# Values of the second half's first two head pairs by seven products, and the routing cut into five parts

## The chip, the cores and the metric

One core of a Trainium2 chip. The metric is the device time of one execution in microseconds; the kernel before takes 2572.6 us (median of 3 runs, 2571.44 to 2572.82).

## The reference

Two layers on x of 8 sequences of 256 tokens, 512 wide, all in float32. What concerns this change is layer 0, whose attention and expert layer both read the layer norm of x:

```
xn  = layernorm(x)                                  # 2048 tokens x 512
q, k, v = silu(xn @ qkv_w.T)                        # 32 heads of 128
attn = scores(q, k) * decay, times v, per head      # causal, blockwise in the reference
gate = sigmoid(xn @ gate_w.T)
x1  = x + (gate * norm(attn)) @ out_w.T + experts(xn)
# experts: logits = xn @ router_w + router_b; softmax, + bias; 2 of 4 groups of 4 experts,
# then the 2 best of the 16 experts per token; each token's two experts are summed with their scores
```

Layer 1 (another attention and a sparse mixture of low-rank pieces) comes after and isn't touched.

## The kernel before

**Numbers.** Every float32 product is made of three passes (`three_passes`, lines 90 to 98: high by high, high by low, low by high), in which each operand is split into a rounded high part and the low rest. ACT makes the high part of a weight (`split`, a cast from `w_in` to `wh`), POOL the low part (`low`, L1805, from `w_in` and `wh` to `wl`). Pieces are 512 columns; a section of weights has four.

**Halves and pairs.** Layer 0's attention runs over two halves h = 0, 1 of 1024 tokens, and in each over 16 pairs of heads. A `Round` is the work for one pair: section 0 (its weights are called "q") makes q and k of the pair's first head, section 1 ("k") those of the second, section 2 ("g") the gate of both. Each section is seven products of a Strassen-Winograd scheme in the order ORDER = (1, 5, 6, 2, 7, 3, 4), each of six matmuls of 128x512 columns. The weights' sums for it are made by POOL (`add_up`, four operations, L492 to L498), and the products' sums by DVE: `summed(r, j, "c")` (L1565) is wanted by product 7 and `summed(r, j, "e")` (L1568) by product 4. ACT copies and activates the results (`take`: "ab", "t5", "a", "e", "c", "b").

**Values.** A regular double is an even and an odd round. In its even round the values of two pairs are made together, as sections 3 and 4 by the same seven products (each of 12 matmuls of 128x256; the weights are v0 and v1, brought by `bring_values` in two transfers each). Only the first double of each half was different: rounds "first" and "second" made their values straight, with `project_v`, four calls per pair of 24 matmuls of 128x256 each.

In half 1, "first" ran: section 0, with the router's matmuls (`route`, `by_token`) inside; project_v 0 and 1; section 1; section 2, with two matmuls for the routing (L1144, L1145: prefix sums and totals of the masks) after its fourth product; scores 0 and 1; project_v 2 and 3. "second" ran three project_v, the scores 0 and 1 and the last project_v at its end. Its v was brought and split for pair 0 at the end of half 0 and the begin of half 1, and q and k of pair 0 too; the gate's weights are brought when half 0's last output matmul is done.

**Order of the work.** Each engine has its program written out by hand in the functions `sync`, `tensor`, `scalar`, `vector` and `gpsimd` inside `half`, each with a `run(r)`; engines meet by counting semaphores, whose counts `Round` works out (`products`, `takes`, `adds`, `splits`, `sums`; `READY` says how many split pieces a section's matmuls wait for; `PLACE` which of four places in `w_in` a section's weights use).

**Routing.** DVE works it out in half 1 for all 2048 tokens, in chains of small operations (`Routing`, lines 136 to 301), each waiting for the one before: in "first", `scores`, (ACT: `exponentials`), `probabilities`, `choose`, `mask_groups` between the sums of section 0 and "c" of section 1; `masks` between "e" of section 1 and "c" of section 2; `count` (which reads the two matmuls' results) after "e" of section 2. In "second", `place` ahead of gated(2), `gates_of_choices` ahead of add_out(0), `experts_of_tiles` after add_out(1). `add_out` takes one of project_out's eight results from one of two banks, and project_out(t) waits for add_out(t - 2).

Of the kernel before, what the change touches and what calls it, by code (L numbers as in the profile page):

```python
# [11 lines left out]
ALU = mybir.AluOpType  # L12
# [121 lines left out]
class Routing:  # L134
# [90 lines left out]
    def count(self, v, prefix, totals):  # L225
# [3 lines left out]
        ab = [x[:, 0:n] for x in self.cmp]  # L229
        c.link(v.tensor_copy(ab[0], totals))  # L230
        incl, free = self.running(v, ab[0], ab[1], E, n)

# [3 lines left out]
        c.link(v.tensor_tensor(above, incl[:, n - E:n].unsqueeze(2).to_broadcast([P, E, NTHR]), thr, ALU.is_gt))  # L236
# [5 lines left out]
        c.link(v.tensor_scalar(tmp, tmp, float(SLOT_T), None, ALU.mult))  # L242
        self.slot = free.rearrange("p (t e) -> p t e", e=E)
# [4 lines left out]
        self.col = tmp  # L248

    def place(self, v, slot_of, ready):  # L250
        c = self.chain
        shape = "p (i t) -> p i t"
        s, col, tile, wrap = (x.rearrange("p t g -> p (t g)")[:, i * 2 * NT:(i + 1) * 2 * NT].rearrange(shape, i=2)
                              for x in (self.gm, self.keep) for i in range(2))
        for i, m in enumerate((self.m0, self.m1)):
            c.link(v.tensor_tensor(self.prod, m, self.slot, ALU.mult))
            c.link(v.tensor_reduce(s[:, i, :], self.prod, AX_X, ALU.add))
# [72 lines left out]

class Round:
# [8 lines left out]
    SPLIT = {"front0": {"v": 2, "q": 6, "k": 10, "g": 14}, "front1": {"q": 4, "k": 8, "v": 10, "g": 14},  # L340
# [3 lines left out]
    SUMMED = {"front0": {"q": 4, "k": 8, "g": 12}, "front1": {"q": 4, "k": 8, "g": 12}, "first": {"q": 4, "k": 8},  # L344
# [4 lines left out]
    PLACE = {"front0": {"q": 0, "k": 1, "g": 2, "v": 3}, "front1": {"q": 0, "k": 1, "g": 2, "v": 3},  # L349
# [3 lines left out]
    def __init__(self, kind, m=0):  # L353
        self.kind, self.m = kind, m
        self.front, self.first, self.second, self.even, self.odd, self.end = (
            kind.startswith(k) for k in ("front", "first", "second", "even", "odd", "end"))
# [3 lines left out]
        self.takes = self.since(0, 22, 44, 30, 48)  # L360
        self.adds = self.since(0, 6, 12, 10, 16)
        self.splits = self.since(14, 24, 40, 22, 36)
        self.sums = self.since(12, 20, 32, 20, 32)

    def since(self, first, second, third, even, both):
# [2471 lines left out]
```

## Time and profile before

| | |
|---|---|
| median of 3 runs | 2572.6 us |
| profiled execution, its time | 2570.18 us |
| its span | 2568.3 us |
| mean granted clock of TensorE | 0.991 |
| busy: PE, DVE, ACT, POOL | 97%, 46%, 45%, 59% |
| matmuls of the values, per pass (`wh,xh` 128x256) | 912 |
| PE's share of the chain that ended last | 85% |

Busy time of TensorE is that of pipelined matmuls, each of which overlaps the next; so a matmul's own duration (400 ns for 512 columns) is longer than the distance to the next one's start. Times in the timelines are microseconds from the span's start. An operation's bracket gives the engine's idle time before it and what ended that. Half 0 fills the time to about 1045 us, half 1 of the attention goes from there.

### The profile page before, as it was taken

Reading aid. Unit: us, or ns where it says so; the run is one execution under the profiler, and the core shown is the slowest. Engines: PE = TensorE matmul, PEld = TensorE weight load, DVE = VectorE, ACT = ScalarE, POOL = GpSimd, SP = SyncE. Lnnn points to the kernel's source line nnn. Section 1 sums busy time; section 2 is a strip of 40 time slices with the busy share of each in tenths; the row PEclk is TensorE's granted clock in tenths of the full one; section 3 lists DMA queues with packets and bytes.
Section 4 is the critical chain, followed back from the end, with each engine's and each line's share of the span. In section 5 each row is a group of like instructions: output and inputs, shape, how many; then the busy total and the mean of one; then the engine's idle time right before and its main releaser. Section 6 shows DMA issues by size and latency. Waiting matters only on the chain.

```text
span 2568.3 us, 39435 instructions
## 1 busy us (share of the span) xinstructions
PE 2495.5 (97%) x13338; PEld 2140.1 (83%) x13338; DVE 1172.4 (46%) x1937; ACT 1152.2 (45%) x2182; POOL 1508.9 (59%) x1523
## 2 busy tenths in 40 slices
PE   7999999999999999999999999999999999969999
PEld 6888888888888888778888888888888888857777
DVE  6333333434343435763334343434343588865443
ACT  5444444444444444443444444444444457733332
POOL 5756656666575754765666766757575578731210
PEclk9999999999999999999999999999999999979999
DMA  4211110111111112211111011111111178931100
GB/s 166 87 48 40 55 63 31 63 47 61 36 58 47 56 40 99 94 48 48 40 55 63 31 63 47 59 35 61 47 56 40 60 245 305 301 101 34 37 29 33
DMA packets 84950, 188.00 MB, mean 73 GB/s; under 512 B 12610, under 2 KB 30674, under 8 KB 84870
## 3 DMA queue, kind: packets, MB, share of 16 engines
q1 hardware_dynamic: 76326, 170.13, 20.0%
q0 software_dynamic: 8544, 16.82, 2.2%
q8 instruction: 48, 0.79, 0.1%
q14 instruction: 32, 0.26, 0.0%
HBM read 168.00 MB, written 26.79 MB: 76 GB/s over the span
## 4 chain that ended last, share of the span: by engine, by line
PE 85%; DVE 7%; ACT 4%; issue 2%; DMA 1%; POOL 1%; ACTq 0%; SPq 0%; DVEq 0%
PE bank L95 24%; PE bank L96 23%; PE bank L97 23%; PE bank L1081 4%; PE bank L1064 4%; PE bank L1082 2%; PE bank L1065 2%; DVE el L2201 2%; ACT exth L2161 1%; ACT eh L2172 1%; ACT eh L2166 1%; DVE ehf L2213 0%; DMA l_stage<-y_slots,slot_of 0%; POOL l_stage L2720 0%; PE bank L539 0%
## 5 line engine op out<-in xcount | busy, mean ns | idle before, releaser
L1805 POOL TENSOR_TENSOR wl<-w_in,wh 128x512 fp32r<-128x512 f32 x510 | 587.7, 1179 | 189.5 <-ACT wh L1348 183.2
L95 PE MATMUL bank<-xh,wh 128*128 128x512 f32 x1400 | 560.7, 400 | 0.7 <-ACT bank L1296 0.7
L97 PE MATMUL bank<-xh,wl 128*128 128x512 f32 x1400 | 546.6, 390 | 0.0
L1823 POOL TENSOR_TENSOR sqacc<-sqacc,sq 128x512 f32<-128x512 f32 x128 | 165.6, 1294 | 379.3 <-ACT sq L1333 368.2
L1348 ACT CAST wh<-w_in 128x512 fp32r<-128x512 f32 x502 | 263.6, 567 | 274.0 <-POOL w_in L498 274.0
L96 PE MATMUL bank<-xl_sums,wh 128*128 128x512 f32 x800 | 315.8, 395 | 0.0
L97 PEld LDWEIGHTS bank<-xh,wl 128*128 128x128 f32 x1400 | 263.0, 188 | 57.3
L95 PEld LDWEIGHTS bank<-xh,wh 128*128 128x128 f32 x1400 | 263.5, 188 | 53.4 <-ACT bank L1296 0.9
L1602 DVE TENSOR_TENSOR acc<-bank,acc 128x512 f32<-128x512 f32 x240 | 165.7, 691 | 299.6 <-PE bank L97 299.6
L95 PE MATMUL bank<-wh,xh 128*128 128x256 f32 x912 | 260.3, 285 | 3.3 <-DVE xl L550 3.3
L96 PE MATMUL bank<-wl,xh 128*128 128x256 f32 x912 | 258.4, 283 | 0.0
L96 PE MATMUL bank<-xl,wh 128*128 128x512 f32 x600 | 234.6, 391 | 0.0
L1559 DVE TENSOR_TENSOR ms<-bank,dcur 128x384 f32<-128x384 f32 x256 | 142.3, 557 | 154.4 <-PE bank L1065 145.2
L95 PE MATMUL bank<-oh,yh 128*128 128x512 f32 x512 | 200.7, 392 | 6.7 <-DVE acc L1600 5.3
L1577 DVE SCALAR_TENSOR_TENSOR yf<-gT,bank 128x512 f32<-128x512 f32 x128 | 88.0, 687 | 249.1 <-PE bank L1082 249.1
L96 PE MATMUL bank<-ol,yh 128*128 128x512 f32 x512 | 200.0, 391 | 0.0
L97 PE MATMUL bank<-oh,yl 128*128 128x512 f32 x512 | 199.8, 390 | 0.0
L1582 DVE SCALAR_TENSOR_TENSOR yl<-yf,little,yh 128x512 fp32r<-128x512 f32 x128 | 131.0, 1023 | 137.0 <-ACT yh L1338 134.8
L1565 DVE TENSOR_TENSOR bank<-bank,t 128x512 f32<-128x512 f32 x128 | 89.5, 699 | 195.3 <-PE bank L97 183.5
L95 PEld LDWEIGHTS bank<-wh,xh 128*128 128x128 f32 x912 | 174.5, 191 | 4.9 <-DVE xl L550 2.1
L96 PEld LDWEIGHTS bank<-xl_sums,wh 128*128 128x128 f32 x800 | 150.6, 188 | 29.6
L96 PEld LDWEIGHTS bank<-wl,xh 128*128 128x128 f32 x912 | 174.5, 191 | 0.7
(354 smaller groups left out, 5394.4 us busy)
## 6 DMA issues: line engine op xcount, KB each, us to landing
w_in<-in_w_pairs_dram SPq DMA_DIRECT2D x100, 512.0 KB, 3.8
o_in<-in_o_pairs_dram SPq DMA_DIRECT2D x32, 512.0 KB, 4.8
eraw<-in_ex_dram SPq DMA_DIRECT2D x31, 513.0 KB, 5.1
y_slots<-ey SPq DMA_DIRECT2D x31, 512.0 KB, 6.0
w_in<-in_w_pairs_dram SPq DMA_DIRECT2D x56, 256.0 KB, 3.1
dcur<-in_decay_dram SPq DMA_DIRECT2D x32, 384.0 KB, 3.0
eraw<-in_ex_dram SPq DMA_DIRECT2D x31, 256.0 KB, 5.1
out_dram<-acc SPq DMA_DIRECT2D x16, 256.0 KB, 2.0
```

The costliest lines, as they stand in the source:

```text
L95: pe.matmul(out, wh, mh, start=start and i == 0, stop=False, skip_group_check=True)
L96: pe.matmul(out, wh, ml, start=False, stop=False, skip_group_check=True)
L97: ins = pe.matmul(out, wl, mh, start=False, stop=stop and i == n - 1, skip_group_check=True)
L1064: pe.matmul(sc[i % 2][:, 0:S], kT[:, hd, s0:s0 + P], qT[:, hd, s0:s0 + S], start=True, stop=True)
L1081: pe.matmul(out, v0, ms[i % 2][:, 0:S], start=True, stop=False, skip_group_check=True)
L1348: a.copy(wh[:, cols], w_in[:, cols]).then_inc(w_hi, 1)
L1559: v.tensor_tensor(ms[i % 2][:], sc[i % 2][:, 0:MC], dcur[:, ITEMS[i][0], :], ALU.mult).then_inc(v_mask, 1)
L1565: v.tensor_tensor(pj[2][:], pj[1][:], t5[:], ALU.add).then_inc(v_c, 1)
L1582: v.scalar_tensor_tensor(yl[g % 2][:], yf[:], nwcur[:, g % 2:g % 2 + 1], yh[g % 2][:].bitcast(F32), ALU.mult, ALU.subtract).then_inc(v_yl, 1)
L1602: v.tensor_tensor(now[:, t, :], op[t % 2][:], now[:, t, :], ALU.add).then_inc(v_acc, 1)
L1805: pool.tensor_tensor(wl[:, cols], w_in[:, cols], wh[:, cols].bitcast(F32), ALU.subtract).then_inc(w_lo, 1)
L1823: pool.tensor_tensor(sqacc[:, c], sqacc[:, c], sq[:], ALU.add).then_inc(p_sq, 1)
```

## The change

In half 1 the rounds "first" and "second" are replaced by Round("even", 0, h=1) and Round("odd", 0, h=1), that is by a regular double with m = 0; half 0 keeps "first" and "second". So in half 1:

- TensorE: no project_v; section 1 directly after section 0; section 2, then section 3 (seven products for the values), products 1 and 5 of section 4, scores 0 and 1, the rest of section 4. The routing's two matmuls go after the fifth product of section 2, not the fourth. The odd round is a regular one.
- v is neither brought at the end of half 0 nor split at the start of half 1. SP brings v0 ahead of o_in, v1 when section 0 is done.
- ACT splits g after the copies "ab" and "t5" of section 1, v0 after "a" and "c" of section 1, v1 around "e" of section 2. POOL's order is: sums for g, sums for v0, low g, low v0, v1, o, token numbers, q, k.
- DVE: `count` is cut in three, and the slots' sum is taken out of `place`. `count_tiles` comes after "e" of section 2, `count_experts` between "c" and "e" of section 3, `count_slots` and `slots_of_choices` after "e" of section 3, `place` after "e" of section 4. In the odd round `gates_of_choices` and `experts_of_tiles` stand together where `place` stood, ahead of gated(2).

The diff, cut to its core:

```diff
-    def count(self, v, prefix, totals):
+    def count_tiles(self, v, totals):
+        ab = [x[:, 0:NT * E] for x in self.cmp]
+        self.chain.link(v.tensor_copy(ab[0], totals))
+        self.incl, self.free = self.running(v, ab[0], ab[1], E, NT * E)
+
+    def count_experts(self, v):
...
+        c.link(v.tensor_tensor(above, self.incl[:, n - E:n].unsqueeze(2).to_broadcast([P, E, NTHR]), thr, ALU.is_gt))
         c.link(v.tensor_reduce(tiles, above, AX_X, ALU.add))
         c.link(v.tensor_copy(ends, tiles))
         self.ends, tmp = self.running(v, ends, tmp, 1, E)
         c.link(v.tensor_tensor(tmp, self.ends, tiles, ALU.subtract))
         c.link(v.tensor_scalar(tmp, tmp, float(SLOT_T), None, ALU.mult))
+        self.col = tmp
+
+    def count_slots(self, v, prefix, totals):
...
         c.link(v.tensor_tensor(free, incl, totals, ALU.subtract))
         c.link(v.tensor_tensor(free, free, prefix, ALU.add))
         c.link(v.tensor_tensor(self.slot, self.slot, tmp.unsqueeze(1).to_broadcast([P, NT, E]), ALU.add))
+
+    def slots_of_choices(self, v):
...
+        for i, m in enumerate((self.m0, self.m1)):
+            c.link(v.tensor_tensor(self.prod, m, self.slot, ALU.mult))
+            c.link(v.tensor_reduce(self.places[0][:, i, :], self.prod, AX_X, ALU.add))
...
-        self.products = self.since(0, 25, 50, 35, 56)
+        self.products = self.since((0, 25, 50), 0, 35, 56)
...
     def ready(self, j):
-        return self.splits + self.READY[self.kind][j]
+        return self.splits + ((-4, 0, 4, 12) if self.first else self.READY[self.kind])[j]
...
             def all_rounds(eng, run):
-                run(FIRST)
-                run(SECOND)
+                run(Round("even", 0, h) if last else Round("first"))
+                run(Round("odd", 0, h) if last else SECOND)
...
             def sync(sp):
                     if r.even:
-                        wait(sp, pe_p, r.products)
+                        if not r.first:
+                            wait(sp, pe_p, r.products)
                         bring_values(sp, r, 0)
...
-                wait(sp, v_yl, 4 * UNITS + 4)
-                bring(sp, FRONT[1], "v", pair_section(0, "v"))
...
             def tensor(pe):
                         section(r, 0, *ORDER[3:])
-                        if last:
-                            project_v(r, 0)
-                            project_v(r, 1)
                         section(r, 1, *ORDER)
-                        section(r, 2, *ORDER[:4])
+                        section(r, 2, *ORDER[:5])
                         if last:
                             masks = router.lg.rearrange("p t e -> p (t e)")
                             wait(pe, v_masks, 1)
...
-                        section(r, 2, *ORDER[4:])
+                        section(r, 2, *ORDER[5:])
...
-                    if r.first and last:
-                        scores(r, 0)
-                        scores(r, 1)
-                        project_v(r, 2)
-                        project_v(r, 3)
-                        return
...
             def scalar(a):
                     if r.first and last:
                         router.exponentials(a)
-                        take_v(r, 0)
-                        take_v(r, 1)
...
                     take(r, 1, "ab")
-                    elif r.odd:
+                    elif r.odd or r.first and last:
                         split(r, "g", 0, 1)
...
                     take(r, 1, "t5")
-                    if r.first and last:
-                        split(FRONT[h], "g", 0, 1, 2, 3)
-                    elif r.odd:
+                    elif r.odd or r.first and last:
                         split(r, "g", 2, 3)
...
                     take(r, 1, "a")
+                    if r.first and last:
+                        split(r, "v0", 0, 1)
...
                     take(r, 1, "c")
+                    if r.first and last:
+                        split(r, "v0", 2, 3)
...
                     take(r, 2, "a")
+                    if r.first and last:
+                        split(r, "v1", 0, 1)
                     take(r, 2, "e")
+                    if r.first and last:
+                        split(r, "v1", 2, 3)
...
             def vector(v):
                         if last:
                             wait(v, pe_pre, 1)
-                            router.count(v, ot[:, 0:NT * E], op[0][:, 0:NT * E])
+                            router.count_tiles(v, op[0][:, 0:NT * E])
...
                         y_low(u, 1)
-                        if second and last:
-                            router.place(v, slot_of, v_slots)
+                        if r.routes:
+                            router.gates_of_choices(v, gate_of)
+                            router.experts_of_tiles(v, expert_of, gates, v_gates)
...
-                        if second and last:
-                            router.gates_of_choices(v, gate_of)
                         add_out(u, 0)
                         summed(r, 1, "c")
                         add_out(u, 1)
-                        if second and last:
-                            router.experts_of_tiles(v, expert_of, gates, v_gates)
...
                         summed(r, 3, "c")
+                        if r.first:
+                            router.count_experts(v)
                         summed(r, 3, "e")
+                        if r.first:
+                            router.count_slots(v, ot[:, 0:NT * E], op[0][:, 0:NT * E])
+                            router.slots_of_choices(v)
                     mask(n, 0)
                     mask(n, 1)
                     if r.even:
                         summed(r, 4, "c")
                         summed(r, 4, "e")
+                        if r.first:
+                            router.place(v, slot_of, v_slots)
...
             def gpsimd(pool):
+                    if r.first:
+                        add(r, "g")
+                        add(r, "v0")
+                        low(r, "g")
+                        low(r, "v0")
+                        add_low(r, "v1")
+                        low_o(r)
...
+                        add_low(r, "q")
+                        add_low(r, "k")
+                        return
...
-                if last:
-                    low(FRONT[1], "v")
-                add_low(FRONT[h], "g")
+                if not last:
+                    add_low(FRONT[h], "g")
```

## Rows read from the trace of the kernel before

**Rows 1.** The page: the span, and TensorE's line of busy times.
```profile
span 2568.3 us, 39435 instructions
PE 2495.5 (97%) x13338; PEld 2140.1 (83%) x13338; DVE 1172.4 (46%) x1937; ACT 1152.2 (45%) x2182; POOL 1508.9 (59%) x1523
```

**Rows 2.** Stretches: length; busy PE, PEld, DVE, ACT, POOL; clock, DMA, GB/s.
```profile
1098.00:1134.00 36.00, 29.90 (x138) 24.99 (x138) 29.27 (x55) 11.11 (x20) 18.75 (x19) 0.91 0.12 42
1166.00:1227.00 61.00, 61.00 (x336) 53.27 (x335) 21.45 (x31) 27.93 (x52) 41.44 (x41) 1.00 0.16 51
```

**Rows 3.** Waits of TensorE from 1045 to 1170 us: total, times, longest.
```profile
PE bank L95 <- DVE acc L1600: 5.3, 1, 5.3
PE bank L1081 <- DVE ms L1559: 0.8, 1, 0.8
PE bank L1144 <- DVE acc L213: 0.7, 1, 0.7
```

**Rows 4.** Timeline of TensorE: start, duration, what, [idle before, releaser].
```profile
1034.21 0.80 PE L95 MATMUL bank<-wh 128*128 128x512 f32 x1 [2.44 <-DVE acc L1755]
...
1061.19 0.28 PE L95 MATMUL bank<-wh,xh 128*128 128x256 f32 x1
...
1066.94 0.40 PE L95 MATMUL bank<-xh,wh 128*128 128x512 f32 x1
...
1082.91 0.70 PE L1144 MATMUL bank<-acc 128*128 128x256 f32 x2 [0.74 <-DVE acc L213]
...
1125.92 0.80 PE L95 MATMUL bank<-oh,yh 128*128 128x512 f32 x1 [5.29 <-DVE acc L1600]
...
1129.78 0.39 PE L95 MATMUL bank<-xh,wh 128*128 128x512 f32 x1
```

**Rows 5.** Timeline of VectorE (DVE), the routing's chains and add_out(0).
```profile
1063.82 0.42 DVE L181 TENSOR_REDUCE acc<-acc 128x16 f32<-128x256 f32 x1 [1.97 <-ACT acc L154]
...
1069.71 0.42 DVE L205 TENSOR_TENSOR acc<-acc 128x256 f32<-128x256 f32 x1
...
1074.62 0.41 DVE L162 TENSOR_REDUCE acc<-acc 128x16 f32<-128x256 f32 x1
...
1081.47 1.39 DVE L213 TENSOR_TENSOR acc<-acc 128x256 f32<-128x256 f32 x1
...
1091.08 0.71 DVE L236 TENSOR_TENSOR acc<-acc 128x128 f32<-128x128 f32 x1
...
1096.61 0.42 DVE L244 TENSOR_TENSOR acc<-acc,bank 128x256 f32<-128x256 f32 x1
...
1111.49 0.96 DVE L256 TENSOR_TENSOR acc<-acc 128x256 f32<-128x256 f32 x1
...
1115.46 0.18 DVE L263 TENSOR_SCALAR acc<-acc 128x32 f32<-128x32 f32 x1
1115.68 1.16 DVE L261 TENSOR_SCALAR acc<-acc 128x32 f32<-128x32 f32 x1
...
1120.76 0.69 DVE L1577 SCALAR_TENSOR_TENSOR yf<-gT,bank 128x512 f32<-128x512 f32 x1
...
1122.29 0.41 DVE L278 TENSOR_TENSOR acc<-acc 128x256 f32<-128x256 f32 x1
...
1125.18 0.69 DVE L1600 COPY acc<-bank 128x512 f32<-128x512 f32 x1
...
1126.98 0.17 DVE L283 COPY acc<-acc 128x16 f32<-128x16 f32 x1
...
1131.04 0.41 DVE L299 TENSOR_TENSOR logits<-acc 128x256 f32<-128x256 f32 x1
```

**Rows 6.** Timeline of GpSimd (POOL): low parts of a section, four operations.
```profile
1071.08 4.48 POOL L1805 TENSOR_TENSOR wl<-w_in,wh 128x512 fp32r<-128x512 f32 x4 [9.27 <-ACT wh L1348]
...
1115.48 4.53 POOL L1805 TENSOR_TENSOR wl<-w_in,wh 128x512 fp32r<-128x512 f32 x4 [0.73 <-ACT wh L1348]
```

**Rows 7.** Timeline of ScalarE (ACT): the casts of g's four pieces.
```profile
1070.38 1.97 ACT L1348 CAST wh<-w_in 128x512 fp32r<-128x512 f32 x4
```

More of the change, by code:

```diff
@@ L348, with __init__, since @@
     READY = {"second": (-6, 0, 4, 6), "even": (-6, -2, 4, 12), "odd": (-4, 0, 4), "end": (-6, -2)}
-    PLACE = {"front0": {"q": 0, "k": 1, "g": 2, "v": 3}, "front1": {"q": 0, "k": 1, "g": 2, "v": 3},
+    PLACE = {"front0": {"q": 0, "k": 1, "g": 2, "v": 3}, "front1": {"q": 0, "k": 1},
              "first": {"q": 0, "k": 1}, "second": {"g": 2, "v": 3, "q": 0, "k": 1},
              "even": {"g": 2, "v0": 3, "v1": 0, "q": 1, "k": 2}, "odd": {"g": 3, "q": 0, "k": 1}}
[L353 to L356, printed above, removed]
+    def __init__(self, kind, m=0, h=0):
+        self.kind, self.m, self.h = kind, m, h
+        self.front, self.second, self.even, self.odd, self.end = (
+            kind.startswith(k) for k in ("front", "second", "even", "odd", "end"))
+        self.first = kind == "first" or self.even and zero(m)
+        self.routes = self.odd and zero(m)
         self.n = UNITS if self.end else m * 2 + 1 if self.odd else m * 2 if self.even else int(self.second)
         self.u = self.n - 1
-        self.products = self.since(0, 25, 50, 35, 56)
[L360 to L365, printed above, removed]
+        self.products = self.since((0, 25, 50), 0, 35, 56)
+        self.takes = self.since((0, 22, 44), 0, 30, 48)
+        self.adds = self.since((0, 6, 12), 0, 10, 16)
+        self.splits = self.since((14, 24, 40), 8, 22, 36)
+        self.sums = self.since((12, 20, 32), 8, 20, 32)
+    def since(self, starts, again, even, both):
         if self.front:
@@ L369, in since @@
         if self.first:
-            return first
+            return again if self.h else starts[0]
         if self.second:
-            return second
+            return starts[1]
         if self.end:
-            return third + both * ((UNITS - 2) // 2)
-        return self.m * both + (third - both + (even if self.odd else 0))
+            return again + both * (UNITS // 2) if self.h else starts[2] + both * ((UNITS - 2) // 2)
+        return self.m * both + ((again if self.h else starts[2] - both) + (even if self.odd else 0))
     def last(self):
@@ L406, in section @@
         return j + (1 if self.odd else 0)
-FRONT = [Round(f"front{h}") for h in range(2)]
-FIRST, SECOND, END = (Round(k) for k in ("first", "second", "end"))
-def zero(n):
-    return isinstance(n, int) and n == 0
+FRONT = [Round(f"front{h}", h=h) for h in range(2)]
+SECOND = Round("second")
 def attention(nc, ctx, x_tiles, xn_dram, x1_dram, token_slots, w_pairs, o_pairs, decay, norm_w, router_w,
@@ L988, in product @@
                                 wait(pe, a_c, taken_n(r, "v", 0))
-                        elif j == 1 and r.first and last:
-                            wait(pe, a_c, taken_n(r, "v", 0))
                         else:
@@ L993, in product @@
                     if k == 5:
-                        if j == 1 and r.first and last:
-                            wait(pe, a_c, taken_n(r, "v", 1))
-                        elif j:
+                        if j:
                             wait(pe, a_c, taken_n(r, "c", j - 1))
@@ L1896, in run @@
                         send(0)
-                    if r.second and last:
+                    if r.routes:
                         pool.wait_ge(v_slots, 1)
@@ L1902, in run @@
                     low_o(r)
-                    if r.second and last:
+                    if r.routes:
                         pool.wait_ge(ids_out, u * 32 + 16)
```

109 lines of the change are left out of this document (45 added, 64 removed).

## The prediction

> **What bounds the kernel now.** I read the page first: TensorE (PE) is busy for 97% of the span [rows 1]. Then the table by stretches: in the ordinary double of rounds PE is busy for all of 61 us at full clock, while in 1098 to 1134 us, inside the first double of the second half, it is busy for 29.9 of 36 us at a granted clock of 0.91 [rows 2]. So a change is worth its TensorE time where PE never waits, and in the first double of half 1, the only place that this diff alters, it is worth that plus or minus waits. The waits of PE there are three: 5.3 us for VectorE's (DVE's) add_out(0), 0.8 for a mask, 0.7 for the routing masks [rows 3]. The timelines of PE, DVE, GpSimd (POOL) and ScalarE (ACT) give the order of the work and its prices [rows 4 to 7].
>
> **What goes.** (a) Values by project_v are 8 calls of 24 matmuls for two pairs, 192; by seven products they are 14 of 12, 168. 48 matmuls of 256 columns ran from 1061.19 to 1066.94 [rows 4], 0.12 us each, so 24 fewer save 2.9 us. (b) The old wait at 1125.92 was 5.3 us idle, and after it nine matmuls took until 1129.78, 3.86 us; at the 0.23 us of the others (66 from 1066.94 to 1082.17, the end of work before 1082.91) they take 2.05. Idle and slow clock (1.2 instead of 2.4 GHz, by the pace and by the granted 0.91 of the stretch) cost 7.1 us together. (c) The wait for the routing masks moves behind one more product, and the mask wait of 0.8 gets cover from seven products and scores: 1.5 us, with a slower matmul or two 1.7. Together 11.7 us at most; new waits at these places are counted below.
>
> **What is moved, free of charge.** ACT's two casts and POOL's two subtractions for the old v at the start of the half go; they lay beside the router's matmuls. SP issues v0 as two transfers ahead of o_in, under 1 us of queue, and v1 once section 0 is through; both land while POOL adds up g, and o_in and dcur are wanted tens of us later. If v0 landed 5 us late, POOL would start g's subtractions late, which is cost 3 below and no new one. The q, k and g transfers of the odd round start at product counts as in any double.
>
> **What the change adds,** in the order of time. All clock times are the old trace's, with the half's start (1045.2) unchanged.
>
> Cost 1, section 1's sum. DVE's order is left as it is: after ACT's exponentials (the op at 1063.82 waits for them) come probabilities, choose and mask_groups, 20 chained ops that end at 1070.13 [rows 5], and only then the sum "c" of section 1, 0.7 us, for which product 7 waits. Before, section 1 started at 1066.94 behind two project_v and that was just in time. Now it starts at 1061.2. Its product 7 is the fifth; four products of six matmuls are 5.5 us, and ACT's exponentials with their table load stand ahead of the copy that the third product wants, 0.5: PE is at product 7 at 1067.2. With the DVE chain as it was PE stands still until 1070.9, 3.7 us. But the chain will not be as it was. Then POOL sat idle for 9.27 us until 1071.08 [rows 6]. Now ACT splits g between the copies of section 1, so POOL's four subtractions for g (1.12 us each) run from 1065.0, two for v0 behind them, to about 1072.4, right beside the chain. What that does is to be seen at 1115.68: the same small tensor_scalar took 0.18 us just before POOL began its subtractions and 1.16 us under them [rows 5, 6]; one DVE op gets through for each POOL op. A reduction is not held (0.41 to 0.42 us in both company and quiet). Laying out the 20 ops so: until 1072.6 six of them that are no reductions each wait out a POOL op, some 0.8 us more for each, the rest run freely, and the chain ends at 1074.9 instead of 1070.1. PE resumes at 1075.6: 8.4 us idle, 0.5 for the late copy, 1.8 of slow clock as in (b), so the first product takes 2.6 us and the second 2.0 instead of 1.4 each. Cost 10.7 us. Bounds: 5.8 (no holding: 3.7 idle, 0.5, and 1.6 of slow clock: after 2.44 us of idle at 1034.21 [rows 4] six matmuls ran at 0.43 us and more instead of 0.23, and eight transposes behind them were 0.2 longer), 12 if more of POOL's ops fall in the chain. I take 10.7, since both rows for the holding show it in full.
>
> The Trainium skill (SBUF — State Buffer, "The single rule") says of this that the port pair DVE shares with GpSimd is an exclusive lock, held for the whole instruction, that a DVE op with two SBUF inputs wants it too, and one with a single input outside certain modes doesn't. The rows agree, and by the rule cost 1 would be as above; without it the 5.8.
>
> Cost 2, the masks. DVE's masks took from 1074.62 to 1082.86, 8.2 us, with POOL's additions and two subtractions beside [rows 5]. Now they start at 1079.3 (product 7 at 1075.6 and the slow clock) and end at 1087.5 in like company, sum c of section 2 at 1088.2. PE, which needs 2.6, 2.0 and 1.4 us for the rest of section 1 and 5.5 for four products of section 2, is there at 1087.1: 1.0 us. Bounds 0 and 2.5. The routing matmuls behind it wait for nothing more.
>
> Cost 3, v1's weights. Section 3 wants all of v0 and v1 split. ACT casts v1's last two pieces behind "e" of section 2, so after g's product 7: DVE's sum 0.7 (as the 0.69 at 1120.76 [rows 5]) with 0.25 to get there, the copy 0.6, two casts 1.0 [rows 7], two subtractions 2.25, 0.2 between engines: 5.0 us. PE has until then the two routing matmuls (0.65) and two products (2.75): 3.4. Cost 1.6, with count_tiles' ops between POOL's 1.7. Bounds 0.8 and 4 (a v0 that is late). This was not there before because v was split whole ahead of the half.
>
> Cost 4, count_experts between "c" and "e" of section 3. Products are now 12 matmuls of 0.12, 1.44 us. "c" ends 5.3 us after section 3 starts (three products, 0.25, 0.7). The same ops took 1091.08 to 1096.61, 5.5 us, beside additions and subtractions [rows 5], as they will have now from the next unit's q. "e" is then done at 11.6; product 4, the seventh, wants it at 8.6: 2.9 idle, 1.6 of slow clock. 4.5 us. Bounds 0.3 (ops at their free 3 us) and 6.
>
> count_slots and slots_of_choices (about 4 us) run while PE does 7 us of products and scores, place (9.2 with the slots before, some 7 without) from the last "e" of the double: PE has 10.8 us of work until it wants section 0's "c", with gated, two masks and that sum, 2.7 us, behind place. Nothing, if place stays under 8; 2 us if not.
>
> Cost 5, what is left at add_out(0). Before, 9.2 us of place (1111.49 to 1120.72) stood ahead of gated(2) and 2.9 of gates (1122.29 to 1125.18) ahead of add_out(0). Now gates and experts (2.9 and, from 1126.98 to 1131.45, 4.5) stand in the first place and nothing in the second [rows 5]: add_out(0) ends 1.8 + 2.9 = 4.7 us earlier, 0.6 behind PE's arrival (1125.92 less 5.29). Experts will have POOL's four g subtractions beside it, where it had additions; I take 1.1 idle and 0.5 of clock, 1.6. Bounds 0.4 and 3.5.
>
> **Sum.** 10.7 + 1.0 + 1.7 + 4.5 + 1.6 = 19.5, less 11.7: 7.8 us longer. The profiled execution took 2570.18 us (1.9 more than its span), so 2578.0 on its own scale. The median of the timed runs is 2572.6, 2.4 higher; on that scale 2580.4.
>
> **Rivals.**
> A. The order costs, the holding does not: POOL's ops miss the chains because they come earlier or later than I place them. Costs 5.8, 1.0, 1.7, 0.3, 0.6, in all 9.4: 2.3 us shorter, 2570.3, no change that can be told. For it: ACT may split g later, and additions (0.73 us) hold less. Against: the g split stands directly behind the copy of section 1, and its weights are in by then. This decides between slower and not: each POOL subtraction that falls in the chain adds about 0.8 us; it turns to slower when three or more fall in the chains of costs 1 and 4 together.
> B. The gain is had nearly whole: beyond A, PE stays at full clock after waits under 4 us and v1 is in time. 9.4 less 1.6 of clock and 1.7: 5.6 shorter, 2567.0. For it: the 0.7 us waits cost next to nothing more. Against: 2.44 us of idle at 1034.21 already left a slow clock [rows 4], and the 3.7 us wait is in the order itself.
> C. A cascade: POOL is late through the double, ACT stands at a split of the next q until the addition is done, place spills into the odd round. Costs at 12, 2.5, 4, 6 and 3.5 and 2 for place less 11.7: 18 longer; half of the way beyond mine is likelier, 2586.
> D. The seven products save nothing, being bound by weight loads: 2.9 more, 2583.3. Against: 0.12 us is the pace of 128x256 matmuls with 128-column loads already.
>
> **Chances.** Forecast 0.53, A 0.25, B 0.07, C 0.13, D 0.02. A measurement here tells 0.2%, 5.1 us, from none. A seventh of the forecast's weight lies within that bound: slower 0.60, same 0.33, faster 0.07. The range 2569.5 to 2586 takes in A and most of C; the forecast's own is 2576 to 2584.
>
> **What would show it.** Right: PE waits some 8 us for sum c (line of "bank<-bank,t") at about 1067, POOL subtractions lie from 1065 beside choose and mask_groups, chain ops of 1.1 us there; a wait of 3 us before product 4 of the first values section; 1 to 2 us at the first project_out pair; 24 fewer matmuls. Wrong: a first wait under 4 us and chain ops at 0.22 (A); no slow clock after it (B); a wait in the odd round's section 0 (C). The forecast as a whole is wrong if the time from 1045.2 to the start of the second double's even round, 1165.4 before, is not some 8 us longer.

## The result and the profile after

The changed kernel takes 2577.53 us, the median of 11 runs (2572.79 to 2581.12); the kernel before took 2571.44 in 11 runs on the same chip (2567.62 to 2574.19). The ratio is 1.0023, with a 95% interval of 1.0014 to 1.0032: slower by 0.23%, some 6 us. I had forecast 7.8 us slower, 2580.4 on the scale of the times shown first.

The page of the profiled execution (2577.96 us), beside [rows 1]: the span, the busy times, and the group of matmuls that the seven products consist of (count, then busy us and mean ns, then idle before them and its releaser).

```profile
span 2576.1 us, 39416 instructions
PE 2492.9 (97%) x13314; PEld 2136.7 (83%) x13314; DVE 1172.1 (45%) x1941; ACT 1156.9 (45%) x2190; POOL 1518.4 (59%) x1535
L95 PE MATMUL bank<-wh,xh 128*128 128x256 f32 x904 | 258.5, 286 | 6.8 <-DVE xl L567 3.4
```

TensorE has 24 matmuls fewer (13338 to 13314) and is busy for 2.6 us less, as meant. The kernel is slower all the same, so it waits more. Where, the waits of TensorE in half 1's first double and the start of the second say (total, times, longest), beside [rows 3]:

```profile
PE bank L95 <- DVE bank L1553: 8.0, 2, 7.7
PE bank L95 <- DVE t L1556: 2.7, 1, 2.7
...
PE bank L95 <- POOL wl L1797: 0.7, 1, 0.7
PE bank L95 <- ACT qT L1309: 0.6, 1, 0.6
PE bank L95 <- DVE acc L1588: 0.6, 1, 0.6
PE bank L1081 <- ACT sq L1324: 0.3, 1, 0.3
PE bank L95 <- ACT bank L1287: 0.2, 1, 0.2
```

L1553 is sum c and L1556 sum e of a section. Of the three old waits (5.3, 0.8, 0.7) the last two are gone and 0.6 of the first is left, at the same copy in add_out (here L1588). One of 7.7 us and one of 2.7 stand in their place, with small ones beside them. The timeline of TensorE has them in order (start, duration, what, [idle before, releaser]):

```profile
1076.22 0.80 PE L95 MATMUL bank<-xh,wh 128*128 128x512 f32 x1 [7.67 <-DVE bank L1553]
...
1079.35 0.40 PE L96 MATMUL bank<-xl,wh 128*128 128x512 f32 x1
...
1087.85 0.50 PE L95 MATMUL bank<-xh,wh 128*128 128x512 f32 x1 [0.31 <-DVE bank L1553]
...
1093.83 0.39 PE L95 MATMUL bank<-wh,xh 128*128 128x256 f32 x1 [0.69 <-POOL wl L1797]
...
1105.40 0.39 PE L95 MATMUL bank<-wh,xh 128*128 128x256 f32 x1 [2.72 <-DVE t L1556]
...
1144.87 0.50 PE L95 MATMUL bank<-oh,yh 128*128 128x512 f32 x1 [0.60 <-DVE acc L1588]
...
1170.82 0.48 PE L95 MATMUL bank<-xh,wh 128*128 128x512 f32 x1
...
1186.61 0.50 PE L95 MATMUL bank<-xh,wh 128*128 128x512 f32 x1 [0.61 <-ACT qT L1309]
```

Two stretches measure the change more sharply than whole runs, which scatter by several us. The first double of half 1, from its first product to the second double's: 1045.23 to 1165.38 before, 120.15 us; 1046.48 to 1170.82 after, 124.34, which is 4.19 longer. And the two doubles up to SP's transfer of v0 in the third, on SP's queue in the kernel before and in the changed one:

```profile
1285.98 0.94 SPq L679 DMA_DIRECT2D w_in<-in_w_pairs_dram  x2
```

```profile
1292.98 0.94 SPq L696 DMA_DIRECT2D w_in<-in_w_pairs_dram  x2
```

That is 240.75 us before and 246.50 after: 5.75 longer, most of the difference of the medians (6.1). From there on the doubles of both kernels keep their distance of 7.0 us (1888.34 against 1895.33 for the same transfer later on). The start of half 1 itself lay anywhere from 1045.2 to 1047.8 in the profiled executions, also among kernels that are alike up to there; that is scatter. "The stretch" below is the second of the two, 240.75 and 246.50.

Why the first wait is so long is on VectorE's timeline, beside the free chain of [rows 5]; then count_experts' end ahead of sum e of section 3:

```profile
1065.07 0.42 DVE L181 TENSOR_REDUCE acc<-acc 128x16 f32<-128x256 f32 x1 [2.81 <-ACT acc L154]
...
1066.27 1.41 DVE L184 TENSOR_TENSOR acc<-acc 128x256 f32<-128x256 f32 x1
...
1068.94 1.19 DVE L164 TENSOR_TENSOR acc<-acc 128x64 f32<-128x64 f32 x1
1070.16 0.22 DVE L165 TENSOR_REDUCE acc<-acc 128x16 f32<-128x64 f32 x1
...
1070.84 1.19 DVE L199 SCALAR_TENSOR_TENSOR acc<-acc 128x64 f32<-128x64 f32 x1
...
1073.28 0.23 DVE L164 TENSOR_TENSOR acc<-acc 128x64 f32<-128x64 f32 x1
...
1075.46 0.70 DVE L1553 TENSOR_TENSOR bank<-bank,t 128x512 f32<-128x512 f32 x1
...
1103.43 1.19 DVE L244 TENSOR_SCALAR acc<-acc 128x16 f32<-128x16 f32 x1
1104.65 0.69 DVE L1556 TENSOR_TENSOR t<-bank,t 128x512 f32<-128x512 f32 x1
```

And GpSimd in the same time, then in the second double:

```profile
1066.08 7.09 POOL L1797 TENSOR_TENSOR wl<-w_in,wh 128x512 fp32r<-128x512 f32 x6 [0.77 <-ACT wh L1339]
...
1178.41 0.19 POOL L1919 COPY token_at<-slot_of 128x2 int32 x1 [2.92 <-DMA token_slots<-token_at]
...
1181.69 0.74 POOL L509 TENSOR_TENSOR w_in<-w_in 128x256 f32<-128x256 f32 x1
```

Six subtractions run from 1066.08 to 1073.17. The same multiplication of 64 columns (L164) takes 1.19 us while they run and 0.23 once they are through; the reduction (L165) takes 0.22 beside them. The chain takes 1065.07 to 1075.43, 10.4 us; it took 6.3 before.

The clock, by stretches (length; busy PE, PEld, DVE, ACT, POOL; granted clock, DMA, GB/s), with the 4 and the 6 us behind the two long waits apart:

```profile
1061.00:1080.00 19.00, 11.16 (x42) 8.44 (x41) 12.41 (x27) 9.02 (x16) 10.06 (x10) 0.82 0.20 69
1076.20:1080.20 4.00, 3.98 (x11) 3.20 (x12) 1.02 (x2) 0.29 (x1) 0.00 (x0) 0.61 0.00 0
...
1105.40:1111.40 6.00, 6.00 (x37) 6.00 (x38) 2.81 (x7) 2.56 (x5) 2.85 (x4) 0.72 0.00 0
```

TensorE is busy for all of both short windows and still slow: 7 matmuls from 1076.22 to 1079.35 in 3.13 us instead of 1.6, and 16 of the values' from 1106.58 at 0.21 us each instead of 0.12.

### The profile page after: what moved, and what is told of

It reads as the page before. It is cut to its first block, busy times and chain, and to the rows that moved or that the text cites. A ratio compares the mean times of both kernels' runs of the same rounds, so it can differ in the third digit from the quotient of the medians.

```text
span 2576.1 us, 39416 instructions
## 1 busy us (share of the span) xinstructions
PE 2492.9 (97%) x13314; PEld 2136.7 (83%) x13314; DVE 1172.1 (45%) x1941; ACT 1156.9 (45%) x2190; POOL 1518.4 (59%) x1535
## 4 chain that ended last, share of the span: by engine, by line
PE 83%; DVE 5%; issue 3%; SPq 2%; ACT 2%; DMA 2%; POOL 2%; ACTq 0%; POOLq 0%; DVEq 0%
PE bank L95 23%; PE bank L96 23%; PE bank L97 23%; PE bank L1081 4%; PE bank L1064 4%; PE bank L1082 2%; PE bank L1065 2%; SPq L2054 1%; DVE el L2200 0%; DMA exin<-xn_rows,ecur 0%; DMA y_slots<-ey 0%; DMA l_stage<-y_slots,slot_of 0%; POOL l_stage L2719 0%; POOL wl L1797 0%; DMA token_slots<-token_at 0%
## 5 line engine op out<-in xcount | busy, mean ns | idle before, releaser
L1797 POOL TENSOR_TENSOR wl<-w_in,wh 128x512 fp32r<-128x512 f32 (+1 forms) x514 | 592.3, 1180 | 197.8 <-ACT wh L1339 193.4
L1553 DVE TENSOR_TENSOR bank<-bank,t 128x512 f32<-128x512 f32 x130 | 91.0, 700 | 198.8 <-PE bank L97 186.2
```

What stands on the lines that cost most here:

```text
L1553: v.tensor_tensor(pj[2][:], pj[1][:], t5[:], ALU.add).then_inc(v_c, 1)
L1797: pool.tensor_tensor(wl[:, cols], w_in[:, cols], wh[:, cols].bitcast(F32), ALU.subtract).then_inc(w_lo, 1)
```

## The experiments

All were run in 5 rounds beside the kernel before. Lines of code are those of the changed kernel unless said otherwise. What I call a kernel's waits are those of TensorE in half 1's first double.

**hold_pool: is it GpSimd's subtractions that hold the chain?** The changed kernel, with the subtractions for g and v0 behind VectorE's mask_groups:

```
+                        pool.wait_ge(router.v_side, 23)
                         low(r, "g")
                         low(r, "v0")
```

> The changed kernel with one wait added: POOL starts the low parts of g and v0 only when DVE has ended mask_groups. My theory (the port is held, POOL's subtractions stretch the chain from 6.3 to 10.4 us): the chain is back at 6.3 us, TensorE's wait for sum c of section 1 falls from 7.7 to about 3.7 us; the six subtractions now lie beside masks, whose 7.3 us become 8 to 9, which gives 1 us back; 3 us shorter than the changed kernel, 3 us longer than the kernel before. Rival (only the order of DVE's work counts, POOL doesn't stretch the chain): the chain stays at 10.4 us, the wait at 7.7, and the time is that of the changed kernel or longer, as POOL is late with v0.

Measured: 2575.62 against 2571.30 us, 1.0016 (1.0007 to 1.0025); stretch 241.35, that is 5.15 less than the changed kernel's. VectorE, TensorE and GpSimd in hold_pool:

```profile
1068.16 0.23 DVE L164 TENSOR_TENSOR acc<-acc 128x64 f32<-128x64 f32 x1
```

```profile
1072.65 0.50 PE L95 MATMUL bank<-xh,wh 128*128 128x512 f32 x1 [3.68 <-DVE bank L1553]
...
1085.34 0.50 PE L95 MATMUL bank<-xh,wh 128*128 128x512 f32 x1 [1.22 <-DVE bank L1553]
...
1102.74 0.39 PE L95 MATMUL bank<-wh,xh 128*128 128x256 f32 x1 [2.62 <-DVE t L1556]
```

```profile
1071.94 9.63 POOL L1797 TENSOR_TENSOR wl<-w_in,wh 128x512 fp32r<-128x512 f32 x8 [5.56 <-DVE acc L205]
```

The same instructions in the same order take 6.3 us from 1065.53 with GpSimd still, against 10.4: 4.0 of the 7.67 us are the holding, and 3.7, what is left, is the order, the very number of the forecast without holding. That is shown. The subtractions then lie beside the masks, and 0.9 of it comes back there (1.22 for 0.31). The gain is larger than I expected, and the windows say why (columns as above; behind the first wait and behind the third):

```profile
1072.60:1078.60 6.00, 5.95 (x19) 4.74 (x20) 3.71 (x6) 1.93 (x4) 6.00 (x6) 0.72 0.00 0
...
1102.70:1108.70 6.00, 5.96 (x47) 5.86 (x48) 3.46 (x9) 3.16 (x6) 3.01 (x5) 1.00 0.00 0
```

Behind its 2.62 us this kernel kept the full clock, where the changed one lost 1.6 us behind 2.72. With the 0.6 us wait in the second double gone too, 4.0 − 0.9 + 0.2 + 1.6 + 0.6 is 5.5 against the 5.15 measured. But the 1.6 us of clock can't be put down to the edit. At about 1035, ahead of half 1, the same matmuls of TensorE wait 2.44 us for VectorE in the kernel before and in the changed one; the slow clock followed in the first and not in the second (columns as above; the 6 us behind the wait, before, then changed):

```profile
1034.21:1040.21 6.00, 6.00 (x24) 4.95 (x25) 6.00 (x11) 2.39 (x5) 1.76 (x3) 0.73 0.27 83
```

```profile
1035.49:1041.49 6.00, 4.92 (x24) 3.86 (x25) 6.00 (x11) 2.93 (x6) 3.26 (x4) 1.00 0.00 0
```

The nine profiled kernels that have the changed kernel's code up to there split in the same way, three slow and six at full clock. Without the 1.6 the gain in the stretch is some 3.5 us, near the 3 that I expected. The interval of the whole time overlaps the changed kernel's; the statement on the gain rests on the traces.

**sums_early: does another order of VectorE help, with the holding left?** Sum c of section 1 ahead of choose, sum e ahead of mask_groups:

```
                             router.probabilities(v)
+                            summed(r, 1, "c")
                             router.choose(v)
+                            summed(r, 1, "e")
                             router.mask_groups(v)
```

> The changed kernel with sum c of section 1 taken ahead of choose and sum e ahead of mask_groups, POOL as it was. My theory (product 7 waits for the order of DVE's program): the 7.7 us wait goes, at most 1 us stays at product 4; but masks now starts at about 1077 at the earliest, beside which TensorE gets to product 7 of section 2 at 1078, so that a wait of 4 to 5 us with 1.5 of slow clock comes there, in place of 0.3: 3 us shorter than the changed kernel, 3 longer than before. Rival (the wait was all of the loss and DVE has room): no wait over 1 us in sections 1 and 2, 9 us shorter than the changed kernel, 3 shorter than before.

Measured: 2578.64 against 2571.30, 1.0030 (1.0019 to 1.0041); stretch 246.41, nothing gained. Both expectations of a gain fell. TensorE in sums_early:

```profile
1073.43 0.50 PE L95 MATMUL bank<-xh,wh 128*128 128x512 f32 x1 [1.37 <-DVE t L1556]
...
1087.20 0.80 PE L95 MATMUL bank<-xh,wh 128*128 128x512 f32 x1 [6.62 <-DVE bank L1553]
```

TensorE goes on and arrives earlier at sum c of section 2, which stands behind the masks, and these behind all that was moved. 7.67 + 0.31 became 1.37 + 6.62, the same 8.0 to 0.01: VectorE has a fixed amount of work to do ahead of the masks' end, and TensorE's products need only one of its sums at a time.

**count_later: the second wait alone.** count_experts behind sum e of section 3 instead of ahead of it:

```
-                        if r.first:
-                            router.count_experts(v)
                         summed(r, 3, "e")
                         if r.first:
+                            router.count_experts(v)
```

> The changed kernel with count_experts after sum e of section 3 instead of ahead of it. My theory: the wait of 2.7 us before product 4 of section 3 goes with the slow clock after it (1.6), and DVE still has 3 us of room before the masks: 4.3 us shorter than the changed kernel, 1.7 longer than before. Rival (the loss is only moved): DVE is late for mask 0 or for sum c of section 4, and at most 1 us is gained.

Measured: 2575.74 against 2571.30, 1.0021 (1.0010 to 1.0032); stretch 246.43, nothing gained. The rival was right, the loss only moved. TensorE in count_later:

```profile
1114.99 0.50 PE L95 MATMUL bank<-wh,xh 128*128 128x256 f32 x1 [2.42 <-DVE bank L1553]
```

**sends_early: what the second double lost.** The writes of the routing table (pick and the two sends) stand beside the additions for q instead of ahead of and behind the low parts of o:

```
+                    if r.routes:
+                        pick(u, n)
+                        send(0)
                     add(r, "v1" if r.even else "q")
+                    if r.routes:
+                        send(1)
...
-                    if r.routes:
-                        pick(u, n)
-                        send(0)
                     low_o(r)
-                    if r.routes:
-                        send(1)
-                        sent(u)
+                    if r.routes:
+                        sent(u)
```

> The changed kernel with the first double's two table writes on POOL put beside the sums of q instead of after the low part of k, and only their end awaited there. My theory: the 0.6 and 0.3 us waits in the second double's first section come from POOL being held by those writes when g is to be added up; they go, with some 0.7 us of refill: 1 to 1.5 us shorter than the changed kernel. Rival (they come from ACT's own order): the waits stay and the time is the same.

Measured: 2576.65 against 2571.30, 1.0027 (1.0017 to 1.0036); stretch 245.39, 1.1 less. No wait is left in the second double, which takes 120.74 us (120.60 before, 122.16 in the changed kernel). So nearly all of its 1.56 us (0.61 and 0.25 of waiting, 0.7 that I did not place in the products around them) come from the table writes. In the changed kernel's last rows of GpSimd above, it waits 2.92 us for one such write and takes up the sums of g at 1181.69; ACT, which stands at g's split, is then late with a copy. In hold_pool, whose table writes stand where they did, the same write is waited for only 2.26 us, the 0.61 is missing, and the second double takes 121.62. The first double of sends_early is 0.31 longer than the changed kernel's, with a wait of 1.29 for v1's weights instead of 0.31 and 0.69. That is not the price of the move: these waits lie at about 1093, and GpSimd comes to the first moved write at 1147.77.

**routing_later: all of the routing behind the sums.** Sums c and e of sections 1 and 2 go in between choose, mask_groups and the masks; scores 0 and 1 stand ahead of section 3; the routing matmuls follow its second product; count_tiles, count_experts and count_slots each move one sum later. The core of it, TensorE then VectorE:

```
+                        scores(r, 0)
+                        scores(r, 1)
+                        section(r, 3, 1, 5)
+                        (wait for the masks, the two routing matmuls)
+                        section(r, 3, *ORDER[2:])
+                        section(r, 4, *ORDER)
...
+                            masking = router.masks(v, v_masks)
+                            summed(r, 2, "c")
+                            next(masking)
+                            summed(r, 2, "e")
+                            next(masking)
```

> The changed kernel with the sums put ahead of the routing's steps all through the double: c of section 1 ahead of choose, e ahead of mask_groups, c of section 2 ahead of masks, e inside masks; the routing's two matmuls after the second product of section 3, scores 0 and 1 ahead of section 3, count_tiles between c and e of section 3, count_experts after e, count_slots between c and e of section 4, the rest after it. ACT and POOL as in the changed kernel. My theory (the loss is which of DVE's sums stands behind which chain): the 7.7 us wait falls to about 1, the 2.7 us wait goes, both stretches of slow clock (1.5 and 1.6) go, the wait for v1's low parts grows from 0.7 to about 2: 11 to 12 us shorter than the changed kernel, 5 to 6 shorter than the one before. Rival (DVE has no room for the chain under POOL's subtractions, as when only section 1's sums were moved): the wait comes back at a sum of section 3 or 4 or at add_out(0), and the time stays over that of the kernel before.

Measured: 2568.69 against 2571.33, 0.9992 (0.9983 to 1.0001); stretch 238.83, 7.7 less than the changed kernel's and 1.9 less than the kernel before. I had expected 11 to 12 less. The waits are 1.37, 0.94, 2.50 and 0.60, and the 0.6 in the second double; the 7.67 with its slow clock is gone for good this time, because TensorE has scores 0 and 1 and two products of section 3 to do instead of standing at the masks. A wait of 2.50 stays, at sum e of section 3, now behind count_tiles.

**routing_later_all: with ScalarE and GpSimd in step.** As routing_later, with the splits of g, v0 and v1 a place earlier on ScalarE, one of g's subtractions ahead of v0's additions, and the table writes as in sends_early:

```
                     take(r, 0, "c")
+                    if r.first and last:
+                        split(r, "g", 0)
...
                         add(r, "g")
+                        low(r, "g", h, (0,))
                         add(r, "v0")
+                        low(r, "g", h, (1, 2, 3))
```

> As the run before (sums ahead of the routing's steps), with ACT's splits of g, v0 and v1 earlier, POOL's first subtraction for g ahead of v0's sums, and the two table writes beside the sums of q. My theory (v1's low parts are what is late then): the wait before section 3 falls by 1 to 2 us and those of the second double (0.9 with 0.7 of refill) go: 2 to 3 us shorter than the run before, 8 to 9 shorter than the kernel before. Rival (more of POOL beside choose and mask_groups stretches them again): a wait of 1 to 3 us comes at the sums of sections 1 and 2 and the time is that of the run before.

Measured: 2569.06 against 2571.33, 0.9986 (0.9977 to 0.9995); stretch 236.97, 3.8 less than before. TensorE in routing_later_all, and the windows behind the first and the third wait:

```profile
1072.73 0.50 PE L95 MATMUL bank<-xh,wh 128*128 128x512 f32 x1 [1.18 <-DVE t L1572]
...
1098.72 0.39 PE L95 MATMUL bank<-wh,xh 128*128 128x256 f32 x1 [2.50 <-DVE t L1572]
```

```profile
1072.70:1078.70 6.00, 5.97 (x26) 4.93 (x27) 5.69 (x10) 2.88 (x5) 5.34 (x7) 1.00 0.30 87
1098.70:1104.70 6.00, 5.98 (x37) 5.98 (x38) 2.96 (x15) 2.58 (x5) 2.95 (x5) 0.72 0.00 0
```

**gates_later: would order alone have helped the kernel before?** The kernel before, with gates_of_choices behind add_out(1) instead of ahead of add_out(0):

```
-                        if second and last:
-                            router.gates_of_choices(v, gate_of)
                         add_out(u, 0)
                         summed(r, 1, "c")
                         add_out(u, 1)
+                        if second and last:
+                            router.gates_of_choices(v, gate_of)
```

> The kernel before with one step moved: gates_of_choices after add_out(1), no longer ahead of add_out(0). It measures what the wait at add_out(0) is worth by itself. My theory: DVE's 2.9 us come off the 5.3 us of idle, the slow clock behind it stays: 2.9 us shorter than the kernel before. Rival (the wait is only put off to a later result): a new wait of 2 to 3 us at one of the next project_out, and the time of before.

Measured: 2571.04 against 2571.33, 0.9992 (0.9982 to 1.0003); stretch 241.06, 0.3 more than before: no difference that can be told. TensorE in gates_later:

```profile
1124.28 0.50 PE L95 MATMUL bank<-oh,yh 128*128 128x512 f32 x1 [2.39 <-DVE acc L1600]
...
1135.71 0.50 PE L95 MATMUL bank<-xh,wh 128*128 128x512 f32 x1 [2.94 <-DVE t L1568]
```

5.3 us became 2.39 and 2.94. The rival was right: here too the routing's time on VectorE only changed the sum that it stood in front of.

**sums_first and sums_first_all: can the last 2.5 us be moved to where nobody waits?** sums_first is routing_later_all with count_tiles and two steps of count_slots behind sum e of section 3, and count_experts between c and e of section 4. sums_first_all adds to it sum e of section 1 ahead of choose's last operation and ScalarE's split of v1 ahead of a copy.

```
                         summed(r, 3, "e")
                         if r.first:
+                            wait(v, pe_pre, 1)
+                            router.count_tiles(v, op[0][:, 0:NT * E])
+                            slots = router.count_slots(v, ot[:, 0:NT * E], op[0][:, 0:NT * E])
+                            next(slots)
...
                         summed(r, 4, "c")
                         if r.first:
+                            router.count_experts(v)
                         summed(r, 4, "e")
```

> On the run with ACT's and POOL's parts (routing_later_all): count_tiles no longer between c and e of section 3 but after e, with the two steps of count_slots that read the banks behind it, then the masks, c of section 4, count_experts, e of section 4, and the rest. My theory: the last long wait, 2.5 us for e of section 3, goes with the 1.6 us of slow clock after it, and at most 1 us comes back at e of section 4: in the stretch from the half's first product to the third double's start 3 to 4 us less, 233 to 234 us against 237.0, and the time 7 to 8 us under the kernel before. Rival (DVE is full there, as when count_experts alone was put later): a wait of over 2 us comes at c or e of section 4 and the stretch stays at 236 or more.

> As sums_first, and e of section 1 ahead of choose's last operation, and ACT's split of v1 ahead of the copy a of section 2. My theory: the waits of 1.2 us before product 4 of section 1 and of 0.9 before section 3 fall to under 0.3 each: 1.5 to 2 us less again, 231 to 232 us in that stretch. Rival (v1's subtractions then lie beside masks and stretch them): the routing's two matmuls or c of section 3 are waited for, and nothing is gained.

Measured: sums_first 2568.94 against 2571.78, 0.9990 (0.9981 to 0.9999), stretch 236.97; sums_first_all 2568.30 against 2571.78, 0.9988 (0.9979 to 0.9997), stretch 237.16. Neither is better than routing_later_all; the rival was right both times. TensorE in sums_first_all, where the first 1.18 + 0.91 of routing_later_all have come apart into 0.16, 0.70, 0.69 and 0.53 and the 2.5 has moved to sum e of section 4, 10 us later:

```profile
1079.31 0.50 PE L95 MATMUL bank<-xh,wh 128*128 128x512 f32 x1 [0.70 <-DVE bank L1581]
...
1083.03 0.50 PE L95 MATMUL bank<-xh,wh 128*128 128x512 f32 x1 [0.69 <-DVE t L1584]
...
1108.75 0.39 PE L95 MATMUL bank<-wh,xh 128*128 128x256 f32 x1 [2.49 <-DVE t L1584]
```

Three versions are faster than both kernels, by 0.10% to 0.14% of the kernel before, with intervals that end just under 1; they can't be told from each other.

## Why the prediction was right, point by point

The direction and the mechanism of the two large costs were right, and the size was 7.8 us against some 6. It came out so near through two errors of opposite sign, and that is luck. By the last of my own signs the forecast fails: I had called it wrong as a whole if the first double did not grow by some 8 us, and it grew by 4.19. What brings the stretch to 5.75 is the second double, where I had forecast nothing.

**The gains, 11.7.** As foreseen: 24 matmuls fewer, and of the three old waits only 0.6 us is left, counted below as cost 5. TensorE's busy time fell by 2.6 us, near the 2.9 of the 24 matmuls.

**Cost 1, 10.7.** Measured 9.4: 0.17 for the late copy, 7.67 idle, 1.5 of slow clock. The first wait of 8 us, the subtractions from 1065 (1066.08) beside the chain and its 1.1 us operations (1.19) are all there, and hold_pool splits the idle time into 3.7 of order and 4.0 of holding, forecast as 3.7 and 4.7.

The Trainium skill (SBUF — State Buffer, "Who interferes with whom", the single rule) has the shared port pair as an exclusive lock. On this chip reductions never want it, operations with two SBUF inputs do, and those with one do not, except that copies, casts and tensor_scalar between SBUF tiles can. The trace agrees: 0.22 and 0.42 us for reductions and 0.70 for the sums that read PSUM, with GpSimd at work or not, against 0.23 and 1.19 for the multiplication with two SBUF inputs. The exception is in the trace too: the tensor_scalar at 1103.43 (L244), with one input, took 1.19 us beside a subtraction, and 0.17 in count_later with none beside it.

**Cost 2, 1.0.** Measured 0.3: the masks took 1079.79 to 1087.06, 7.3 us, where I had kept the old 8.2 with its company; GpSimd stood still for the first 2.1 of them. Under its subtractions in hold_pool they took 9.2, and the wait was 1.22. The company is what sizes it.

**Cost 3, 1.7.** Measured 0.7. The low parts of v1 were ready a little earlier than I placed them; I did not resolve by which step.

**Cost 4, 4.5.** Measured 4.3: 2.72 idle where 2.9 was forecast, 1.6 of slow clock. That the slow clock came with it was luck: hold_pool had 2.62 idle and none, and the 2.44 us of [rows 4], from which I had it that such a wait slows the clock, did not slow it in the changed kernel.

**Cost 5, 1.6.** Measured 0.6, and no slow clock. This is the 0.6 that the sum gave before I added 0.5 for GpSimd's subtractions beside experts. Two of them did lie there, but gates and experts took 7.45 us together (1135.12 to 1142.57), the 2.9 and 4.5 that they had taken before. Behind so short a wait no slow clock came. place, which I had at 7 us and as costing nothing, took 4.7 (1117.72 to 1122.4); GpSimd worked for only 2.4 of them.

Together 15.3 against 19.5, less 11.7: 3.6. The first double is 4.19 longer; of the 0.6 left over a part is the first matmul behind each wait, 0.1 us longer, and the rest I did not place.

**The step that was missing** is the second double, which I took for an ordinary one ("nothing" beyond the first). It is 1.56 us longer because the table writes, now late in the routing's five parts, stand on GpSimd's queue ahead of g's sums; sends_early shows it. My rule that each queue past which a step moves counts was applied to VectorE and ScalarE, and not to GpSimd's sends. Costs 2, 3 and 5 together were too high by 2.7 and cost 1 by 1.3, this was too low by 1.6, and so 7.8 came out where the stretch shows 5.75.

**The rivals.** A, the order without the holding, is refuted by the 1.19 us rows. hold_pool makes it real for cost 1 alone: its first double is 0.4 us shorter than the kernel before's, where A had 2.3, because count_experts kept three subtractions beside it there and 2.62 us of idle time, which A had at 0.3. The full price of A was not measured. B falls with A, and its full clock behind waits under 4 us falls with the 0.72 behind 2.72 us here and behind 3.68 in hold_pool. C did not come: place stayed under 8 us and nothing spilled into the odd round. D falls with the 2.6 us less of busy time.

What stays open: whether the better order would do as well without the seven products was not tried, so the 3.8 us of routing_later_all are not divided between them. The gates_later run says only that moving one part in the old kernel brings nothing. Nor was it tried to take work off VectorE in this stretch, which is what the experiments point to.

## What to carry to other kernels

A chain of small operations between the sums that TensorE waits for costs what it takes beside the work that shares its ports, not what it takes alone; look at what the other engine will be doing by then, and price the chain in that company. Cutting such a chain into parts and moving them past one sum after another moves the wait with it (7.67 + 0.31 to 1.37 + 6.62; 2.72 to 2.42; 5.29 to 2.39 + 2.94): here it paid only where TensorE had work that needs none of these sums, the scores and two products ahead of the routing matmuls. And every queue on which a moved step issues something is to be followed until it is steady again, past the round in which the change lies.

## What the runs showed of the hardware

**The price of the slow clock does not depend on the idle time.** It was 1.5 to 1.8 us after 2.72, 3.68, 5.29 and 7.67 us of idleness alike. After the long ones (5.29, 6.62, 7.67) the first matmul is already slow (0.80 us); after 2.72 and 3.68 TensorE runs at full pace for 1.2 and 1.0 us first and is slow then. That is no rule for short waits: after the 2.42 us in count_later it is slow from the second matmul on. The first slow and the first fast matmul behind the 3.68 us in hold_pool:

```profile
1073.68 0.61 PE L96 MATMUL bank<-xl_sums,wh 128*128 128x512 f32 x1
...
1077.08 0.42 PE L95 MATMUL bank<-xh,wh 128*128 128x512 f32 x1
```

**Idle times of 2.4 to 2.7 us go either way.** The granted clock in the 6 us behind them was 0.72 after 2.42, 2.49, 2.50 (twice), 2.54 and 2.72 (three times), and 1.00 after 2.39 and 2.62. Nor does the code decide it. The wait of 2.43 to 2.47 us at about 1035, the same in the nine kernels that are alike up to there, was followed by 0.72 or 0.73 in hold_pool, count_later and sends_early and by 1.00 in the other six; of the kernel before and gates_later, alike there too, the first shows 0.73 and the second 1.00. Behind waits of up to 1.37 us in the stretch it was 1.00 each time, but what lies between is not safe: near the kernel's start, at some 27 us, a wait of 1.84 to 1.86 us was followed by 0.72 in nine of the eleven profiled kernels. So a forecast that counts on shortening a wait from 2.7 to 2.6 can gain 1.6 us or nothing by it, and where two profiled executions differ by one such 1.6, the edit between them need not be the reason.

**Beside GpSimd's subtractions, one VectorE operation with two SBUF inputs gets through for each.** Beside the six subtractions, 1.18 us each, six operations of the chain were held. Those of 64 columns took 0.40 to 0.93 or 1.19 us instead of 0.23, by how much of the current subtraction was left; the whole chain of 20 took 10.4 us instead of 6.3.
